# Scans of the state-space layers: the projections of the next unit in slot 4 of the preceding direction, and the per-unit side work in new slots

## The reference, cut to what matters

```python
xz = jnp.einsum('bhwc,ec->bhwe', x, in_w);  xa, z = jnp.split(xz, 2, axis=-1)
xc = silu(dwconv3x3(transpose(xa), conv_w, conv_b))
xs = # xc read in 4 directions: rows, columns, and both reversed
x_dbl = jnp.einsum('bkdl,kcd->bkcl', xs, xproj_w)          # -> dts, Bs, Cs
delta = jax.nn.softplus(dts + dt_b)
h = exp(delta * A) * h + delta * Bs * xs                    # 8 states, along L = 4096
ys = einsum(h, Cs)                                          # summed over states
y = ys of the 4 directions, put back in place and added, + Ds * xs
out = (layernorm(y, ln_g, ln_b) * silu(z)) @ out_w.T
```

## Time and profile before

| | us |
|---|---|
| median of 3 runs (lowest, highest) | 7589.84 (7584.07, 7591.32) |
| profiled execution, its own time | 7577.74 |
| span of the profile | 7575.6 |
| the scans' loop, units 0 to 63 | 3171.2 to 6245.5 |
| DVE, ACT, POOL, PE busy in that stretch | 2902, 2372, 2707, 2543 |

### The profile page before, as it was taken

One profiled execution on the slowest core, in us unless ns is written; L12 is line 12 of the kernel. 1 busy time (PEld: TensorE's weight loads), 2 busy tenths in 40 slices (PEclk: granted clock), 3 DMA queues, 4 the chain that ended last, 5 costly groups with the idle time before them and its releaser, 6 DMA issues. The chain is left out here.

```text
span 7575.6 us, 105356 instructions
## 1 busy us (share of the span) xinstructions
PE 6033.1 (80%) x18336; PEld 2087.1 (28%) x18336; DVE 6379.9 (84%) x7490; ACT 5233.5 (69%) x10936; POOL 5446.2 (72%) x4289
## 2 busy tenths in 40 slices
PE   6888878878888883688888888888888777898696
PEld 2222222222222221222222222222222113488252
DVE  6999999999999997299999999999999994533636
ACT  6777777777777773477777787777777774322756
POOL 5888888888888883288888888888888881000606
PEclk8999999999999996788999999999989878997888
DMA  3544444444445445487787788777888773246222
GB/s 87 114 106 101 108 113 104 103 111 113 102 106 114 106 101 125 115 189 180 186 188 185 185 188 187 186 185 184 185 189 186 182 167 94 110 153 194 80 60 77
DMA packets 584409, 1051.09 MB, mean 139 GB/s; under 512 B 105735, under 2 KB 140732, under 8 KB 579100
## 3 DMA queue, kind: packets, MB, share of 16 engines
q1 hardware_dynamic: 584060, 1047.70, 57.7%
HBM read 857.89 MB, written 189.54 MB: 138 GB/s over the span
## 5 line engine op out<-in xcount | busy, mean ns | idle before, releaser
L1629 POOL TENSOR_TENSOR scan_prod<-scan_hs,scan_BC_rep 128x512 f32<-128x512 f32 x1536 | 1937.7, 1271 | 303.1 <-DVE scan_hs L1553 292.8
L644 POOL TENSOR_TENSOR mamba_prod<-mamba_hs,mamba_BC_rep 128x512 f32<-128x512 f32 x1536 | 1904.8, 1271 | 36.9 <-DVE mamba_hs L602 33.5
L602 DVE TENSOR_TENSOR_SCAN mamba_hs<-mamba_dA,mamba_carry,mamba_dbx 128x512 f32<-128x512 f32 x1152 | 1435.8, 1271 | 37.5 <-ACT mamba_dA L526 18.4
L1173 PE MATMUL scan_u_rep<-scan_du,scan_sel 96*128 96x512 f32 x1536 | 949.1, 703 | 502.8 <-DVE scan_hs L1553 502.6
L526 ACT ACTIVATE mamba_dA<-mamba_delta_rep,mamba_a_neg 128x512 f32<-128x512 f32 x1536 | 1088.9, 710 | 211.1 <-DMA mamba_delta_rep<-delta_units 103.9
L1398 ACT ACTIVATE scan_dA<-scan_delta_rep,scan_a_neg 128x512 f32<-128x512 f32 x1536 | 1092.1, 712 | 87.6 <-DVE scan_hs L1553 77.0
L1553 DVE TENSOR_TENSOR_SCAN scan_hs<-scan_dA,scan_carry,scan_dbx_even 128x512 f32<-128x512 f32 x768 | 975.8, 1271 | 72.7 <-ACT scan_dA L1398 45.2
L1553 DVE TENSOR_TENSOR_SCAN scan_hs<-scan_dA,scan_carry,scan_u_rep 128x512 f32<-128x512 f32 x768 | 976.3, 1271 | 61.5 <-ACT scan_carry L1378 56.8
L581 DVE TENSOR_TENSOR mamba_dbx<-mamba_u_rep,mamba_BC_rep 128x512 f32<-128x512 f32 x1152 | 780.9, 678 | 83.2 <-PE mamba_u_rep L325 52.7
L336 PE MATMUL mamba_y<-mamba_prod,mamba_gather 128*32 128x512 f32 x3072 | 591.5, 679 | 318.6 <-POOL mamba_prod L644 318.6
L1952 POOL TENSOR_TENSOR ffn_sq<-ffn_xm 96x512 f32<-96x512 f32 x64 | 66.2, 1035 | 952.1 <-DVE ffn_xm L1920 942.3
(11 more groups left out here) (283 smaller groups left out, 10596.8 us busy)
## 6 DMA issues: line engine op xcount, KB each, us to landing
scan_BC_rep<-proj_rows SPq DMA_DIRECT2D x1024, 256.0 KB, 6.4
scan_delta_rep<-proj_rows SPq DMA_DIRECT2D x1024, 192.0 KB, 3.6
mamba_BC_rep<-bc_units SPq DMA_DIRECT2D x512, 256.0 KB, 7.5
mamba_delta_rep<-delta_units SPq DMA_DIRECT2D x512, 192.0 KB, 5.5
proj_rows<-scan_dbc SPq DMA_DIRECT2D x256, 224.0 KB, 3.4
delta_units<-mamba_delta SPq DMA_DIRECT2D x128, 192.0 KB, 5.7
by_n<-fin_res SPq DMA_DIRECT2D x32, 768.0 KB, 3.2
fmid_src<-by_n SPq DMA_DIRECT2D x32, 768.0 KB, 5.2
```

The lines of the kernel that those rows point to most:

```text
L602: nc.vector.tensor_tensor_scan(hs[:, s % RING_H], dA[:, s % RING_A], dbx_bank(s)[:], carry[:, bass.ds(at, 1)], op0=ALU.mult, op1=ALU.add). ...
L644: pool.tensor_tensor(prod[:, (G * u + s) % RING_P], hs[:, s % RING_H], BC_rep[:, u, QUADS + s % QUADS], ALU.mult).then_inc(s_prod, 1)
L1173: nc.tensor.matmul(u_rep[c][:], sel[:, c], du[:, k], start=True, stop=True).then_inc(s_rep_u, 1)
L1629: pool.tensor_tensor(prod[:, (G * k + s) % RING_P], hs[:, (G * k + s) % RING_H], BC_rep[:, k, 2 + s % 2], ALU.mult).then_inc(s_prod, 1)
```

## The change

Every edit moves a step to another slot. On PE, `project` no longer stands in slot 0 of a direction (for 3 directions ahead) but in slot 4 (for 4 directions ahead), ahead of the taps of that slot; one more projection is made before the loop. The taps move from slots 2 to 7 to slots 3 to 9, `var` from 16 to 14, `project_out` from 21 to 20. On ACT, `copy_z` moves from 1 to 4, the silus from 12 to 13, `start_y` from 14 to 19, `square` from 15 to 16, `affine` from 20 to 21; `rsqrt` stays in 18 and `evict_out` in 23. On POOL, `normalise` moves from slot 17 to slot 15, ahead of `add_softplus`, and `gate` from 20 to 19. On SP, `load_out` and its wait for the store before it move from the head of the unit to its direction k = 1.

```diff
-    CONV_TAPS = {2: (0, 1), 3: (1, 3), 4: (3, 4), 5: (4, 6), 6: (6, 7), 7: (7, 9)}
+    CONV_TAPS = {3: (0, 1), 4: (1, 2), 5: (2, 4), 6: (4, 5), 7: (5, 6), 8: (6, 8), 9: (8, 9)}
...
-                    if out == 1:
-                        sp.wait_ge(s_store, stored)
-                        load_out(at_res)
...
+                    if k == 1 and out == 1:
+                        sp.wait_ge(s_store, stored)
+                        load_out(at_res)
...
+                        if s == 4 and has_next:
+                            pe.wait_ge(s_bc, j + PRE + 1)
+                            pe.wait_ge(s_relu, j + PRE + 1)
+                            project(nxt_lay, k, *nxt)
...
-                        if has_out and at == 16:
+                        if has_out and at == 14:
                             var(f)
-                        if has_out and at == 21:
-                            project_out(f, out)
-
-                        if ahead and s == 0:
-                            pe.wait_ge(s_bc, j + PRE)
-                            pe.wait_ge(s_relu, j + PRE)
-                            project(lay if k + PRE < D else nxt_lay, kp, image, r, rows)
...
+                        if has_out and at == 20:
+                            project_out(f, out)
...
-                        if has_out and at == 1:
+                        if has_out and at == 4:
                             copy_z(f)
-                        if at == 12:
+                        if at == 13:
...
-                        if has_conv and at == 14:
+                        if has_conv and at == 19:
...
-                        if has_out and at == 15:
+                        if has_out and at == 16:
                             square(f)
...
-                        if has_out and at == 20:
+                        if has_out and at == 21:
                             affine(f, out)
...
+                        if has_out and k == 2 and s == 3:
+                            normalise(f)
                         if s == 3 and ahead:
                             add_softplus(j + PRE, (k + PRE) % D)
...
-                        if has_out and k == 2 and s == 5:
-                            normalise(f)
-                        if has_out and k == 3 and s == 2:
+                        if has_out and k == 3 and s == 1:
                             gate(f)
```

More of the change, by code:

```diff
@@ L1187, in body @@
                 has_conv, has_out, has_next = conv is not None, out is not None, nxt_lay is not None
-                now = values(pe, n // CH % 2, n % CH, (n // CH + 1) * CH)
                 nxt = values(pe, (n + 1) // CH % 2, (n + 1) % CH, ((n + 1) // CH + 1) * CH) if has_next else None
@@ L1194, in body @@
                     j = D * n + k
-                    ahead = has_next or k + PRE < D
-                    image, r, rows = (now if k + PRE < D else nxt) if ahead else (None,) * 3
-                    kp = (k + PRE) % D
                     for s in range(G):
@@ L1210, in body @@
                         if has_conv and at in CONV_TAPS:
-                            if at == 2:
+                            if at == 3:
                                 pe.wait_ge(s_xc, n + CH)
@@ L1247, in _ @@
             pe.wait_ge(s_xc, CH)
-            for k in range(PRE):
+            for k in range(PRE + 1):
                 wait(pe, s_bc, k)
```

## The result

The changed kernel takes 7604.23 us, the median of 9 runs (7597.67 to 7620.03); the kernel before, run beside it, 7589.84 us (9 runs, 7580.25 to 7592.1). The ratio is 1.0024, 95% interval 1.0014 to 1.0034: some 18 us slower, just beyond what can be told from no change. The forecast was 7522 us, 68 us faster, in a range that ended at 7600.

What follows compares the result with a forecast made beforehand. DVE bounds the kernel: 44.8 us of work a unit plus waits, mostly for late ACT. Stretch changes of -18, -22, -11 and -17 us sum to -68, from 7590 to 7522 us; range 7475 to 7600.

Steps and rivals of the forecast that it cites:

- slot 14: Stall of DVE's scan behind the silu block, as ACT's `dA` starts 5.7 us late against a 5.4 lead: 0.3 us.
- 46 us and no faster: Loads and stores in the second layer: with SP's wait gone, they let a unit go at about 46 us at best.
- sign that the prediction named for its own failure: Prediction wrong if the taps end over 5 us after scan 9, or POOL's idling is above 5 us a unit.
- taps and silu: PE's eight products from scan 7's end take 6.9 us; last tap 3.6 us after scan 9; ACT waits 2.9 us.
- slot 17: Stall of DVE's scan after ACT's softplus and square in slots 15 and 16 lose 1 us more than they give: 0.7 us.
- rival (a): Slower: taps too late, PE's clock halved between slots 7 and 9; slower from 1.4 us later on; 7685 us, 12%.
- the accumulation: DVE's accumulation between scans 17 and 18: no stall forecast, 0 us.
- PE's lower clock in some of these places: Allowance in the sum for PE running slower, tied to no single slot: 0.2 us a unit.
- slot 0: Stall from the late chain through `gate`, `project_out` and `evict_out`: 0.6 us a unit, 1.4 in the second layer.
- slot 22: Stall through `copy_bc`, as POOL is behind after idling for `rsqrt`: 0.5 us a unit.
- rival (c): All hidden: ACT's lead absorbs the silu wait, POOL recovers, only transfers bound; -121 us, 7469 us, 8%.

Runs made afterwards that it cites:

- e4: The changed kernel with `var`, `normalise`, `gate` and `project_out` back in their old slots (16, 17, 20, 21); 7558.5 us, ratio 0.9968 to the kernel before.
- e7: The changed kernel with only the last tap moved, from slot 9 to slot 8; 7503.1 us, ratio 0.9895 to the kernel before.
- e9: The changed kernel with the taps spread over slots 3 to 8, a single one in 8 and none in 9; 7466.5 us, ratio 0.9849 to the kernel before.
- e12: The changed kernel with the taps in slots 3 to 8, run once more for a profile; 7471.5 us, ratio 0.9853 to the kernel before.
- e3: The changed kernel with the taps back in slots 2 to 7 and `copy_z` back in slot 1; 7480.5 us, ratio 0.9867 to the kernel before.

## Why the prediction was wrong

**Right.** The projection is off the path (317.1 us of ACT's wait to 6.6 in the whole program), what is late next is POOL's product at `copy_bc` (175.5 us in units 8-39, some 1.8 a wait), and the moved load shortens SP's gap. DVE stalls at slots 14, 17 and 0 in place of 10, 13 and 22. POOL idles 3.5 us a unit at `normalise` (197.2 / 56), forecast 3.7. The silu block lasts 3.81 us again (4545.65 to 4549.46, with 1.29 from the table load to the activation): the drain of the Trainium skill's "ScalarE: Activation LUTs", "What ACT_TABLE_LOAD costs", isn't in this trace either. The first stretch fell less than forecast, 46.4 us and not 45.3: slot 14 loses 0.8 us there too, where the forecast had no stall, and even without it none of the kernels with the projection moved went under 45.5. The last fell more, 45.5 and not 46.3, so the transfers' "46 us and no faster" is no floor for those units. Neither sign that the prediction named for its own failure came: the taps end 4.3 us after scan 9 and not over 5, POOL idles 3.5 us and not over 5.

**The step that failed** is *taps and silu*: "8 x 0.86 = 6.9, less 3.54, or 3.4 and 0.2 of latency, 3.6 us after scan 9 ends". The mechanism was right, and the size was off: the eight take 7.8 us, the tap ends 4.3 us after, and ACT starts at 4.4. The 0.86 came from three taps in a row; the new order puts two gatherings and a `u_rep` between the taps, and the steps around these take 0.95 to 0.99. Slot 14 lost 1.0 to 1.1 us and not 0.3, slot 17 1.0 and not 0.7. Since the lead was already spent there, every tenth was paid, as rival (a) said. (The 1.1 us that the prediction gives for before belong to slot 13; slot 14 lost nothing then.)

**The term that was missing** is the accumulation, 0 in the sum, 0.8 and 0.7 us measured. `var` was moved ahead of the gathering of slot 14, with a wait for `square`, which stands behind the silus on ACT. I costed `var` as a position, and not as a wait with the gathering and DVE's accumulation queued behind it. The sum's 0.2 us for "PE's lower clock in some of these places" was an allowance with no place of its own; the clock took 0.7 to 0.8 us here alone, and about 1.1 at slot 0 in 40-55. Rival (a) named PE's lower clock as the danger, but between slots 7 and 9, where the clock stayed at 1.00; it fell where PE had idled for `square` and for `gate`. And (a) priced itself from 1.4 us of lateness on; 0.7 us was enough, because three places hang on the last tap and not one. The late tap alone had not turned the sign: e4, with the tap as late and no stall at the accumulation, is 24 us faster than the kernel before.

The loop by stretches: forecast 362, 1507, 766 and 370 us; measured 371.3, 1554.4, 805.4 and 363.7. Of the 88 us between them 86 are in units 8 to 55. In 8-39 a unit is 1.5 us over: slot 14 +0.7, slot 17 +0.3, the accumulation +0.8, slot 0 +0.1, slot 22 -0.4, and -0.2 for the sum's clock term, which is inside the others here, with 0.1 in small parts. In 40-55 it is 2.4 over: slot 14 +0.8, slot 17 +0.3, the accumulation +0.7, slot 0 +1.0, slot 22 -0.3, and the same -0.2 and 0.1. e7 shows that all of the middle terms go with one product. e9's 7466.5 us is near rival (c)'s 7469, but that is in part luck: (c) needed the eviction in time, and slot 0 still loses 1.8 us in e12's units 40-55; its stretches are 46.0, 46.2, 47.0 and 45.5 us a unit, where (c) had 45 and then 46.3.

## What to carry to other kernels

Before a step is moved later, ask what lead the engine that waits for it has left at that place: with none left, an error in the cost of eight products (0.9 us here) goes into the time in full, and may set off further waits. Price a product by a row in which it stands between others of the same kind as in the new order, not in a run of its own kind. And a wait that is moved ahead of other work on an in-order engine needs a term of its own, for the work behind it and for the clock of that work.

## What the runs showed of the hardware

- A product of two passes over 512 columns takes 0.86 us (two passes of 0.43) when a tap or a projection follows a tap, and 0.95 to 0.99 us around a gathering and behind most `u_rep`, at the full granted clock in both cases. It is so in the kernel before as well: there the 83 steps from a tap to a gathering in units 8 to 63 have a median of 0.95, the 240 from tap to tap 0.86. Why is not shown.
- TensorE's granted clock was 0.50 (1.2 GHz) right behind a wait of 3.89 us in unit 12, but in unit 28, behind a wait of 3.72 us, `var` still took 1.07 us and the gathering behind it 1.56. With waits of some 1.5 us at this place (e7) `var` was slowed once, to 1.45 us. In e3 it took 2.02 us in unit 9 with no wait right before it; PE had idled 1.98 us before the `u_rep` ahead of it. Where exactly it falls differs from unit to unit of one execution, and the runs don't settle why.
- Transfers come to 189 to 195 GB/s in e12's first three stretches (195 in units 40-55, at 47.0 us a unit), against 176 to 186 in the earlier trace rows.
